# Householder steps of a 256 x 256 tridiagonalization: the order of VectorE's four block updates in the two-block steps

## The reference

```python
h = jnp.maximum(_layernorm(x), 0.0)
x = x + _L0_gnn_ref(h, adj, W1, b1, W2, b2)
h = jnp.maximum(_layernorm(x), 0.0)
x = x + _L1_gnn_ref(h, adj, Wg0, bg0, Wg1, bg1, Wih, Whh, bih, bhh)

# in _L0_gnn_ref: the eigenvectors of the normalized Laplacian
L_norm = d_inv_sqrt[:, None] * (jnp.diag(deg) - A) * d_inv_sqrt[None, :]
_, U = jnp.linalg.eigh(L_norm)
agg = jnp.einsum('mn,bnd->bmd', U.T, features)
out = jax.nn.relu(agg @ W1 + b1) @ W2 + b2
return jnp.einsum('nm,bmd->bnd', U, out)
```

## Time and profile before

| | |
|---|---|
| median of 3 runs | 1594.41 us (1592.82 to 1594.41) |
| the profiled execution | 1591.15 us |
| its span | 1589.4 us |
| VectorE busy | 1247.3 us, 78% |
| TensorE matmul busy | 1232.0 us, 78% |
| ScalarE busy | 648.1 us, 41% |
| GpSimd (POOL) busy | 396.0 us, 25% |

### The profile page before, as it was taken

One profiled execution on the slowest core, in us unless ns is written; L12 is line 12 of the kernel. 1 busy time (PEld: TensorE's weight loads), 2 busy tenths in 40 slices (PEclk: granted clock), 3 DMA queues, 4 the chain that ended last, 5 costly groups with the idle time before them and its releaser, 6 DMA issues.

```text
span 1589.4 us, 25248 instructions
## 1 busy us (share of the span) xinstructions
PE 1232.0 (78%) x5744; PEld 1014.7 (64%) x5747; DVE 1247.3 (78%) x6154; ACT 648.1 (41%) x2370; POOL 396.0 (25%) x2138
## 2 busy tenths in 40 slices
PE   5888889999976667777354554365999999999997
PEld 4666777777765555555233333163778789999997
DVE  7999998888888888888999999996772355556555
ACT  2333333333433434322121222251334677878775
POOL 5333334444445555555200000002000010000000
PEclk9999999999999999999967776687999999999999
DMA  7000000000000000000000000000000000001011
GB/s 172 2 1 1 1 1 1 1 1 2 1 1 1 1 1 1 1 1 1 1 0 1 1 0 1 0 1 0 1 1 1 0 1 1 1 1 28 1 28 54
DMA packets 23405, 12.65 MB, mean 8 GB/s; under 512 B 5075, under 2 KB 22230, under 8 KB 23254
## 3 DMA queue, kind: packets, MB, share of 16 engines
q1 hardware_dynamic: 23254, 11.03, 2.8%
HBM read 6.83 MB, written 4.19 MB: 7 GB/s over the span
## 4 chain that ended last, share of the span: by engine, by line
DVE 49%; PE 32%; issue 9%; POOL 7%; ACT 2%; DVEq 1%; POOLq 0%
PE bank L836 8%; DVE A L1058 5%; PE bank L838 5%; PE bank L845 4%; DVE RC L1146 4%; DVE O L1154 4%; DVE zc L1052 3%; DVE wk L1042 3%; DVE pa L1142 3%; DVE O L1150 3%; DVE junk L1005 3%; PE pair L836 2%; PE pair L689 2%; DVE A L1048 2%; DVE NG L1020 2%
## 5 line engine op out<-in xcount | busy, mean ns | idle before, releaser
L484 ACT ACTIVATE ncp<-pc,RC 128x2 f32<-128x2 f32 (+1 forms) x254 | 74.9, 295 | 324.1 <-DVE RC L1026 324.1
L693 PE MATMUL bank<-O,y 128*128 128x2 f32 x510 | 142.3, 349 | 65.3 <-DVE y L1005 59.9
L623 ACT ACTIVATE H<-bank,gate_b 128x128 f32<-128x128 f32 (+2 forms) x468 | 163.4, 436 | 56.8 <-PE bank L838 40.3
L678 PE MATMUL bank<-ident,O 128*128 128x128 f32 x382 | 148.2, 457 | 47.9 <-DVE O L1035 35.4
L693 PEld LDWEIGHTS bank<-O,y 128*128 128x128 f32 x510 | 127.7, 311 | 77.7 <-issue 72.0
L836 PE MATMUL bank<-O,WlT 128*128 128x128 f32 (+1 forms) x672 | 146.9, 328 | 7.8 <-DVE O L1422 5.5
L701 PE MATMUL pair<-ident,pc 128*128 128x128 f32 x381 | 147.9, 457 | 5.5 <-DVE pc L1024 2.3
L678 PEld LDWEIGHTS bank<-ident,O 128*128 128x128 f32 x382 | 60.2, 198 | 136.0 <-DVE O L1035 136.0
L768 PE MATMUL bank<-chg,fold 128*128 128x512 bf16 x61 | 28.3, 585 | 139.2 <-DVE chg L1104 139.2
L319 POOL TENSOR_TENSOR ym<-y,below 128x2 f32<-128x2 f32 (+1 forms) x254 | 49.1, 193 | 330.0 <-DVE y L1013 232.1
L836 PEld LDWEIGHTS bank<-O,WlT 128*128 128x128 f32 x672 | 112.7, 192 | 18.4 <-ACT H L623 9.2
(11 more groups left out here) (435 smaller groups left out, 3463.7 us busy)
## 6 DMA issues: line engine op xcount, KB each, us to landing
X<-in_x SPq DMA_DIRECT2D x2, 2048.0 KB, 13.2
out<-X SPq DMA_DIRECT2D x32, 128.0 KB, 1.9
adj_sb<-in_adj SPq DMA_DIRECT2D x1, 256.0 KB, 3.0
W1s<-in_L_gnn_W SPq DMA_DIRECT2D x1, 64.0 KB, 11.1
W2s<-in_L_gnn_W SPq DMA_DIRECT2D x1, 64.0 KB, 4.2
Wg0s<-in_L_gnn_Wg SPq DMA_DIRECT2D x1, 64.0 KB, 3.9
Wg1s<-in_L_gnn_Wg SPq DMA_DIRECT2D x1, 64.0 KB, 3.9
Wl<-in_L_gnn_Wih SPq DMA_DIRECT2D x1, 0.5 KB, 6.8
```

What stands on the lines that cost most here:

```text
L484: a(ncp[:, bs], pc[:, bs], ACT.Identity, scale=RC[:, k, 1:2]).then_inc(S["ncp_ready"], 1)
L623: ins = a(gates[:, q, i, 0:n], gate_at(p, q, i), fn, bias=gate_b[:, p - 1, i:i + 1])
L678: ins = nc.tensor.transpose(xb[:, b * P:(b + 1) * P], R[:, b, k, 0:1].to_broadcast([P, P]), idf)
L693: ins = mm(sb_[:, 0:2], y[:, 1:2].to_broadcast([P, P]), R[:, 1, k, :], start=True, stop=(k >= P - 1))
```

## The change

In the two-block steps the order of four updates and z is changed. Before: lower block by p, z, upper block by p, lower block by z, upper block by z. After: lower block by p, z, lower block by z, upper block by p, upper block by z. The loops over the two blocks are written out for it. The waits are the same, each ahead of the same instruction. In one-block steps the order is what it was.

```diff
-                for b in reversed(range(2)):
-                    e = P if b == 0 else N
-                    if b in todo:
-                        stt(out=A[:, b, c0 + 1:e], in0=prow[:, c0 + 1:e], scalar=cx[:, b:b + 1], in1=A[:, b, c0 + 1:e], op0=ALU.mult, op1=ALU.add).then_inc(S["add1" if b else "add0"], 1)
-                    if b == 1:
-                        dve.wait_ge(S["ncp_ready"], k + 1)
-                        dve.wait_ge(S["w_ready"], k + 1)
-                        stt(out=zc[:, bs], in0=cx[:, bs], scalar=wk[:], in1=ncp[:, bs], op0=ALU.mult, op1=ALU.subtract, reverse1=True).then_inc(S["z_ready"], 1)
+                if 1 in todo:
+                    stt(out=A[:, 1, c0 + 1:N], in0=prow[:, c0 + 1:N], scalar=cx[:, 1:2], in1=A[:, 1, c0 + 1:N], op0=ALU.mult, op1=ALU.add).then_inc(S["add1"], 1)
+                dve.wait_ge(S["ncp_ready"], k + 1)
+                dve.wait_ge(S["w_ready"], k + 1)
+                stt(out=zc[:, bs], in0=cx[:, bs], scalar=wk[:], in1=ncp[:, bs], op0=ALU.mult, op1=ALU.subtract, reverse1=True).then_inc(S["z_ready"], 1)
                 dve.wait_ge(S["z_ready"], k + 1)
-                for b in todo:
-                    e = P if b == 0 else N
-                    if b == 0:
-                        dve.wait_ge(S["add0"], k + 1)
-                    stt(out=A[:, b, c0 + 1:e], in0=xb[:, c0 + 1:e], scalar=zc[:, b:b + 1], in1=A[:, b, c0 + 1:e], op0=ALU.mult, op1=ALU.add).then_inc(S["upd1" if b else "upd0"], 1)
+                if 1 in todo:
+                    stt(out=A[:, 1, c0 + 1:N], in0=xb[:, c0 + 1:N], scalar=zc[:, 1:2], in1=A[:, 1, c0 + 1:N], op0=ALU.mult, op1=ALU.add).then_inc(S["upd1"], 1)
+                if 0 in todo:
+                    stt(out=A[:, 0, c0 + 1:P], in0=prow[:, c0 + 1:P], scalar=cx[:, 0:1], in1=A[:, 0, c0 + 1:P], op0=ALU.mult, op1=ALU.add).then_inc(S["add0"], 1)
+                    dve.wait_ge(S["add0"], k + 1)
+                    stt(out=A[:, 0, c0 + 1:P], in0=xb[:, c0 + 1:P], scalar=zc[:, 0:1], in1=A[:, 0, c0 + 1:P], op0=ALU.mult, op1=ALU.add).then_inc(S["upd0"], 1)
```

## The result

The changed kernel takes 1616.24 us (median of four runs) against 1594.41 of the kernel before: the ratio is 1.0137, 95% interval 1.0116 to 1.0158, so 18.5 to 25.2 us slower. One of the four runs was a slow one, 1680.67 us at a lower granted clock (0.888 for 0.943 to 0.945), and without it the median is 1614.61, 20.2 over the kernel before. In a later pairing on one chip it was 1616.93 against 1591.03, ratio 1.0158 (1.0144 to 1.0171). The profiled execution took 1613.98 with a span of 1612.3, which is 22.9 over the span of before. I had forecast 1619.4, and 25.0 slower.

What follows compares the result with a forecast made beforehand. Early two-block steps were taken as bound by VectorE from zc to y0, the last ones by waiting for TensorE's y01. 30.2 us added on VectorE less 5.2 returned is 25.0 slower, on the median 1594.41: 1619.4 us, range 1611 to 1629.

Steps and rivals of the forecast that it cites:

- (a): Two-block steps, VectorE: lower block's update by z directly behind zc exposes a wait, 0.12 us more per step.
- (b): Two-block steps, VectorE: upper block's update by z directly behind its update by p, 0.12 us more per step.
- The bound I had set around the pair that the earlier trace didn't contain: Upper block's update by p, then by z: from full overlap, 0.12 less per step, to a 0.11 gap, 0.07 more.
- (c): Everything else between zc and half keeps its length; zc to half becomes 1.22 at k = 17, 0.89 at k = 125.
- (d): Late steps: L1013's wait for y01 closes, but L693 and L696 then end last; 5.2 us back, bounds 0 and 9.0.
- the waits cost nothing: Rival: VectorE spaces dependent pairs like independent ones and y01 comes earlier; 1589.2 us, faster, 4%.
- half of it: Rival: on VectorE (a) is paid and (b) isn't; 15.1 less the 5.2 given back, 1604.3 us, 6%.
- TensorE takes the gain wholly or not at all: Late steps: return is 9.0 (1615.6 us) or 0 (1624.6 us); the forecast's own bounds, within its 77%.
- The waits cost more: Rival: one VectorE pair takes the 0.11 gap instead of 0.04, 8.8 more, 1628.2 us; both, 1637.0; 10%.

Runs made afterwards that it cites:

- the first two runs of the experiments: Changed kernel with the upper block's update by p ahead of zc: 1608.85 us; changed kernel with a small instruction behind zc and one behind add0: 1615.18 us.

## Why the prediction was right, and what it missed

(a) and (b), the two pairs: forecast 0.12 us each, 1.22 from zc to half at k = 17 and 0.89 at k = 125; measured 1.23 and 0.90, in sum 31.3 us for 30.2. The trace shows both, in every two-block step. A run shows the first by itself: zc, upd1 alone costs 15.6 in the stage (15.1 forecast). No run has the second alone; it is what is left of the 31.3, 15.7. That both are idle time is shown by the run that fills them at no cost. The bound I had set around the pair that the earlier trace rows didn't contain (none, or a 0.11 gap) was not needed: the upper block's update by z starts 0.04 behind the end of the update by p that it waits for, with 126 columns and with one.

(c) Held: between half and the reads nothing moved.

(d) What the late steps give back: forecast 5.2, bounds 0 and 9.0. The path that I named, from the first read over L693 and L696 to x, is there: x comes 1.58 after the first read in step 125 (1.56 forecast), and the term from that read to x is 5.0. But the wait's end gave back 2.0 more between x and the next zc, which no step of mine had. It lies between the start of x (L1035) and that of wk behind it, 21.6 us in sum before and 19.6 after; from wk to zc it is 57.7 in both. And x itself got shorter by as much: its lengths add up to 31.0 us before and 29.1 after.

The traces also show what x collides with: POOL's product vt (L332), which no step of mine looked at. Step 120 of the kernel before, with a long x:

```profile
439.12 0.26 DVE L1035 SCALAR_TENSOR_TENSOR O<-cx,gqn,tm 128x2 f32<-128x2 f32 x1
439.18 0.19 POOL L332 TENSOR_TENSOR vt<-ident,NG 128x2 f32<-128x2 f32 x1
```

Step 125 of the kernel before, with a short x and a long vt:

```profile
455.40 0.22 DVE L1035 SCALAR_TENSOR_TENSOR O<-cx,gqn,tm 128x2 f32<-128x2 f32 x1
455.46 0.22 POOL L332 TENSOR_TENSOR vt<-ident,NG 128x2 f32<-128x2 f32 x1
```

Step 120 of the changed kernel, both short:

```profile
463.19 0.19 POOL L332 TENSOR_TENSOR vt<-ident,NG 128x2 f32<-128x2 f32 x1
463.21 0.22 DVE L1035 SCALAR_TENSOR_TENSOR O<-cx,gqn,tm 128x2 f32<-128x2 f32 x1
```

Where vt starts 0.02 to 0.06 after x, one of the two is stretched: either x, and then it ends 0.01 after vt does, or vt, to 0.22. Where vt starts sooner, both are short. Of the steps 0 to 126 of the kernel before, 78 have a long x (over 0.225), 41 a long vt and 8 neither; of the changed kernel 44, 28 and 55. No step of either trace falls outside this. In the late steps of before x waits for POOL's tm (L326) and starts 0.08 after POOL's next product (L327), so that vt always falls into it; in the changed kernel x waits for gqn, up to about 0.09 later against POOL, so that vt starts when x does or before it. So the 2.0 belong to the same change of path as the 5.0. That fits the sum too: with y01 free in the order of before, x's lengths add up to 29.4. Which of the two gives way when they collide, and what it is that they share, no run here tells.

The sum of the stage was then 24.3 for 25.0, with 1.0 too little on VectorE and 1.8 too little given back. The point forecast of 1619.4 was 3.2 over the first median. The medians lie 21.8 apart in the first pairing and 25.9 in the second, on either side of the stage's 24.3; the stretch behind the stage varies by some 4 us from run to run, so I read no more into that.

The rivals: *the waits cost nothing* and *half of it* fell with the first two runs of the experiments and the trace of the changed kernel. *TensorE takes the gain wholly or not at all* fell with the traces: 7.0 of 9.0 came back, and x comes 1.58 after the first read in both orders once y01 is early. *The waits cost more*: not for these pairs, which have a single wait each; but the gap that I had taken as its price is real, and I had its condition only in part. Each such gap has two waits ahead of it, and moving one of them away took 0.10 from each late step; yet L1013 has two as well and no such gap.

## What to carry to other kernels

An order of instructions on one engine that puts a consumer directly behind its producer pays for the lost overlap and the wait, here 0.12 us each time, whatever the number of columns; read it from a stretch of the same trace where the pair already stands so. An independent instruction between the two is free there, so look for real work to put in, and before moving something earlier for another engine's sake, check in how many steps that engine is waited for at all, and which path ends last once it isn't.

## What the runs showed of the hardware

- On VectorE an instruction that doesn't wait started 0.07 to 0.09 us before the end of the one ahead; one that waits by a single semaphore for the one directly ahead started 0.03 to 0.04 after its end, in each of the 126 steps, with the producer at 2 columns (zc) and at 126 down to 1 (add0).
- With two waits in a row ahead of it, of which the second ended last, an instruction of VectorE started 0.10 (L1020, L1035) or 0.14 (the reduction) after the end of what it waited for. Where the first ended last (L1013 of the changed kernel) it was 0.04, and where both had long been over, nothing.
- TensorE's second fp32 product (L696, two passes of loads) started 0.38 to 0.40 us after the first one (L693) in nearly every step of the changed kernel, with its input ready 0.05 to 0.17 before.
- Where POOL's small product (L332) started 0.02 to 0.06 after VectorE's (L1035), one of the two took longer: up to 0.26 for 0.22 on VectorE, or 0.22 for 0.19 on POOL. Which one, was not found.
